# Maxima in two halves of heads, with exponentials among the last scores; normalisation on GpSimd; the gate's first layer in bf16 parts on TensorE; new engine orders

## The chip, the cores and the metric

One core of a Trainium2 chip. The metric is the device time of one execution in microseconds. Five engines run their own instruction queues in order: TensorE (PE), VectorE (DVE), ScalarE (ACT), GpSimd (POOL) and SyncE (SP), which here only issues the DMAs. They meet at semaphores.

## What is computed

Sixteen items (B = 16), each a matrix of 256 positions by 256 features, go through four residual steps:

```python
x = x + einsum(x, W0[subject]) + b0[subject]              # a linear layer chosen per item
x = x + zX*lap_x(x) + zY*lap_y(x) + zR*x*(1 - x)          # a Laplacian step
# attention, 16 heads of 16: q, k_self, v_self from side, k, v of the past from x
score_prev = where(mask, q @ k.T, -inf) / 4               # 256 x 256 per head
score_self = sum(q * k_self) / 4                          # one more column
weights = softmax(concat(score_prev, score_self))
x = x + (weights[..., :-1] @ v + weights[..., -1:] * v_self) @ Wo + bo
# three experts, dense 256 -> 1024 -> 256 with relu: s0, s1 shared, eo chosen per item
w = softmax(relu(concat(eo[:, 0], s0[:, 0], s1[:, 0]) @ g1) @ g2)
x = x + eo*w[0] + s0*w[1] + s1*w[2]
```

The gate g1 sees position 0 alone: a vector of 768 against a 768 x 256 matrix.

## The kernel before

The work is features on partitions, two chunks of 128 (C = 2), 256 positions in the free dimension. A float32 product is made in three matmuls of split operands (hi·hi, hi·lo, lo·hi, function `product`, lines 488 to 490). Scores are bf16 products of stacked parts: `q_rows` and `k_rows` hold three-part splits of q and k in bands of 16 rows, placed there by DMAs (`place`, line 386), with a mask row and, for the second pass, three rows with minus the maximum.

The heads are gone through twice. Stages S0 to S15 (line 586) make scores with queries on partitions, and VectorE takes each row's maximum (line 930). After S15 the maxima are joined with the self score (933), subtracted (935), transposed on TensorE (`mT`, 591), split in three bf16 rows by VectorE (941 to 944) and brought into `q_rows` by three DMAs (421). Stages E0 to E15 (597) make scores less maximum with keys on partitions; ScalarE takes the exponential, once in float32 (777) and for even heads once more in float16 (781); for odd heads VectorE makes the float16 part (950). What is left, `prob_lo`, is made by VectorE for odd heads (951) and by GpSimd for even ones (1136). The products with V, `attend(h)` (539, 540), stand three heads later: E_h is followed by `attend(h - 3)`, and `pvend` holds the last three. `attend(8)` reuses the banks of the first eight heads and waits for `pv_freed`, which VectorE raises after it has summed a bank (stage `half`, 961 and 963). Stages `norm` and `att` normalise (970 to 974); `aT` transposes, `wo` projects.

The experts are H0 to H11 (a hidden block of 128x512, 12 matmuls) and P0 to P11 (12 matmuls into the output banks), four of each per expert. After an H, ScalarE makes `hid_hi` (821) and VectorE `hid_lo` (1004), and P needs both. After P3, P7 and P11 ScalarE copies the output (801). The third expert is chosen per item: SP loads its first matrix into `raw`, stage `wi_part` splits it (ScalarE 794, GpSimd 1086), then SP loads the second into the same `raw` (`wo_load`, line 370), and `wo_part0` to `wo_part3` split that. Stages gate0 to gate2 form the gate's first layer on VectorE (1014 to 1019); TensorE sums it with ones (655); `relu`, `logits`, `mix`, `scale` follow.

One loop turn holds the front of item i, the attention's second part of item i-1 and experts of items i-1 and i-2. The order in a turn is a list, `BODY`, written out by hand: a front order with `STEP` saying what follows each stage. All engines follow it, VectorE with the later places of `DVE_LATER`. Front stages use two PSUM banks alternately (`front_bank`): a stage waits until the one two places earlier in `USES` has been read, by ScalarE (`freed_act`) or VectorE (`freed_dve`). TensorE's turn reads, from S0: S0 S1 P1 S2 S3 H3 S4 S5 P2 S6 S7 H4 S8 S9 P3 S10 S11 H5 S12 S13 P4 S14 S15 H6 mT P5 H7 P6 E0 E1 H8 E2 P7 E3 E4 H9 E5 E6 P8 E7 to E10 H10 E11 E12 P9 E13 E14 H11 E15 P10 pvend x1 P11 q aT gate ks logits lap wo vs kp vp H0 self H1 P0 H2. ScalarE's `wi_part` stands behind S1, `wo_load` behind S3, `wo_part0` behind H5.

Before the loop VectorE splits the linear weights, and in the first item's turn the shared experts' weights are loaded and split in eight pieces (`SHARED_AT`).

Of the kernel before, what the change touches and what calls it, by code (L numbers as in the profile page):

```python
# [80 lines left out]
DVE_BODY = list(BODY)  # L87
for name, later in DVE_LATER.items():
    DVE_BODY.remove(name)
    DVE_BODY.insert(DVE_BODY.index(later) + 1, name)  # L90
LAGS = (EARLY + ATTENTION[:FIRST_HALF] + ["x_parts", "w_parts", "s_parts", "x1_parts", "x2_parts", "react", "self"],
        ATTENTION[FIRST_HALF:] + ["half", "norm", "pvend", "att", "aT", "wo", "x3_parts"]
        + [x for stage in ATTENTION[:FIRST_HALF] for x in AFTER.get(stage, []) if x not in ("sum", "self", "store")])
LAG = {x: 0 if x in LAGS[0] else 1 if x in LAGS[1] else 2 for x in BODY}
# [1112 lines left out]
```

## Time and profile before

| | |
|---|---|
| median of 3 runs | 1146.45 us (1146.3 to 1146.51) |
| profiled execution | 1148.39 us, span 1146.8 us |
| TensorE busy | 988.7 us, 86% |
| VectorE busy | 868.9 us, 76% |
| ScalarE busy | 603.8 us, 53% |
| GpSimd busy | 568.5 us, 50% |
| DMA queue's share | 32% |
| mean granted TensorE clock | 0.967 of full |

The chain that ended last is made of TensorE 38%, VectorE 30%, issue 12%, DMA 10%, ScalarE 6%. Read the engine shares first, then the waits of the busiest engine, and then, in order of time, one turn out of the middle: sixteen items make sixteen nearly equal turns, with a first one that has no experts beside it (TensorE's busy tenths there are 5, 5 and 8 in slices two to four, with the clock granted at half for most of it) and a last one that has little else.

### The profile page before, as it was taken

How to read it: one execution, taken by the hardware profiler on the slowest of the kernel's cores; microseconds unless marked ns; L12 is line 12 of the kernel's file. 1: busy time of each engine (PE TensorE's matmuls, PEld its weight loads, DVE VectorE, ACT ScalarE, POOL GpSimd, SP SyncE). 2: the span in 40 equal slices, each digit the busy share in tenths (PEclk: the TensorE clock that was granted, in tenths of full speed). 3: DMA queues.
4: the chain of work that ended last, by engine and by line, in shares of the span. 5: the costliest groups of instructions: out<-in, count | busy, mean ns of one | idle time of the engine just before them, and what ended most of it. 6: DMA issues, size and time to landing. Idle time of an engine off the chain costs nothing.

```text
span 1146.8 us, 27267 instructions
## 1 busy us (share of the span) xinstructions
PE 988.7 (86%) x9456; PEld 922.6 (80%) x9456; DVE 868.9 (76%) x1710; ACT 603.8 (53%) x1177; POOL 568.5 (50%) x432
## 2 busy tenths in 40 slices
PE   4558988998898999889899888989898898989886
PEld 4228888888888888888888888888888888888785
DVE  3576787877778787777878777787877778787733
ACT  3354654646565464656546455655645565554532
POOL 6573636455463645446364544636454463644422
PEclk9559999999999999999999999999999999999988
DMA  4725233251524324152422415242241524223110
GB/s 133 161 74 84 76 70 65 69 92 37 92 74 72 74 61 88 37 92 74 76 80 55 83 37 92 74 80 86 48 80 37 92 74 83 83 55 73 39 46 10
DMA packets 79339, 83.46 MB, mean 73 GB/s; under 512 B 11444, under 2 KB 74708, under 8 KB 79316
## 3 DMA queue, kind: packets, MB, share of 16 engines
q1 hardware_dynamic: 79316, 83.15, 32.0%
q8 instruction: 14, 0.23, 0.1%
q14 instruction: 9, 0.07, 0.0%
HBM read 53.37 MB, written 4.20 MB: 50 GB/s over the span
## 4 chain that ended last, share of the span: by engine, by line
PE 38%; DVE 30%; issue 12%; DMA 10%; ACT 6%; SPq 2%; POOL 1%; DVEq 1%; ACTq 0%; POOLq 0%
DMA k_rows<-prob_lo 7%; PE front L586 4%; DVE prob_hi L950 4%; PE out L488 4%; PE out L489 4%; PE out L490 4%; PE hid L488 4%; PE hid L490 4%; PE hid L489 4%; PE front L597 3%; DVE s_max L930 3%; DMA q_rows<-max_rows 3%; DVE hid_lo L1004 2%; PE front L488 2%; SPq L421 2%
## 5 line engine op out<-in xcount | busy, mean ns | idle before, releaser
L821 ACT ACTIVATE hid_hi<-hid 128x512 fp32r<-128x512 f32 x192 | 114.6, 597 | 251.5 <-PE hid L490 250.8
L488 PE MATMUL out<-hid_hi,exp_hi 128*128 128x256 f32 x768 | 230.1, 300 | 14.7 <-DVE hid_lo L1004 14.6
L1136 POOL TENSOR_TENSOR prob_lo<-prob,prob_hi 128x512 f16<-128x512 f32 x128 | 162.9, 1273 | 137.3 <-ACT prob_hi L781 137.3
L488 PE MATMUL hid<-x_hi,exp_hi 128*128 128x256 f32 x768 | 226.7, 295 | 2.2 <-DVE x_lo L1000 2.2
L930 DVE TENSOR_REDUCE s_max<-front 128x2 f32<-128x512 f32 x256 | 165.2, 688 | 77.0 <-PE front L586 76.0
L489 PE MATMUL out<-hid_lo,exp_hi 128*128 128x256 f32 x768 | 216.8, 282 | 0.0
L490 PE MATMUL out<-hid_hi,exp_lo 128*128 128x256 f32 x768 | 216.5, 282 | 0.0
L489 PE MATMUL hid<-x_lo,exp_hi 128*128 128x256 f32 x768 | 214.5, 279 | 0.0
L490 PE MATMUL hid<-x_hi,exp_lo 128*128 128x256 f32 x768 | 214.4, 279 | 0.0
L1086 POOL TENSOR_TENSOR exp_lo<-raw,exp_hi 128x512 fp32r<-128x512 f32 (+1 forms) x80 | 154.8, 1946 | 104.5 <-ACT exp_hi L794 104.3
L777 ACT ACTIVATE prob<-front 128x512 f32<-128x512 f32 x256 | 146.8, 600 | 63.4 <-PE front L597 61.7
L1004 DVE SCALAR_TENSOR_TENSOR hid_lo<-hid,hid_hi 128x512 fp32r<-128x512 f32 x192 | 131.0, 682 | 48.8 <-ACT hid_hi L821 48.8
L488 PEld LDWEIGHTS out<-hid_hi,exp_hi 128*128 128x128 f32 x768 | 146.1, 190 | 19.5 <-DVE hid_lo L1004 18.2
L488 PEld LDWEIGHTS hid<-x_hi,exp_hi 128*128 128x128 f32 x768 | 145.5, 189 | 3.3 <-DVE x_lo L1000 2.5
L489 PEld LDWEIGHTS out<-hid_lo,exp_hi 128*128 128x128 f32 x768 | 146.5, 191 | 0.0
L490 PEld LDWEIGHTS out<-hid_hi,exp_lo 128*128 128x128 f32 x768 | 146.3, 190 | 0.0
L489 PEld LDWEIGHTS hid<-x_lo,exp_hi 128*128 128x128 f32 x768 | 145.7, 190 | 0.0
L490 PEld LDWEIGHTS hid<-x_hi,exp_lo 128*128 128x128 f32 x768 | 145.0, 189 | 0.0
L950 DVE CAST prob_hi<-prob 128x512 f16<-128x512 f32 x128 | 86.2, 674 | 55.0 <-ACT prob L777 51.4
L597 PE MATMUL front<-q_rows,k_rows 100*128 100x256 bf16 x512 | 100.0, 283 | 27.3 <-DMA q_rows<-max_rows 18.5
L539 PE MATMUL pv<-v_cols,prob_hi 128*128 128x49 bf16 x1024 | 89.6, 187 | 32.2 <-DVE prob_lo L951 19.4
L539 PEld LDWEIGHTS pv<-v_cols,prob_hi 128*128 128x128 f16 x1024 | 72.4, 97 | 50.2 <-DVE prob_lo L951 25.2
(153 smaller groups left out, 2280.7 us busy)
## 6 DMA issues: line engine op xcount, KB each, us to landing
raw<-in_wi SPq DMA_DIRECT2D x16, 1024.0 KB, 4.9
raw<-in_wo SPq DMA_DIRECT2D x16, 1024.0 KB, 5.5
q_rows<-prob_hi SPq DMA_DIRECT2D x96, 128.0 KB, 4.2
k_rows<-prob_lo SPq DMA_DIRECT2D x96, 128.0 KB, 4.6
x_raw<-in_x SPq DMA_DIRECT2D x17, 256.0 KB, 2.7
w_raw<-in_w SPq DMA_DIRECT2D x17, 256.0 KB, 2.8
s_raw<-in_side SPq DMA_DIRECT2D x17, 256.0 KB, 3.5
out<-e_out SPq DMA_DIRECT2D x16, 256.0 KB, 2.2
```

What stands on the lines that cost most here:

```text
L488: nc.tensor.matmul(acc, w_hi, a_hi, start=first, stop=False)
L489: nc.tensor.matmul(acc, w_hi, a_lo, start=False, stop=False)
L490: return nc.tensor.matmul(acc, w_lo, a_hi, start=False, stop=last)
L539: nc.tensor.matmul(acc, prob_hi[:, h % NPROB, at:at + P], v_cols[:, k, h, :], start=(k == 0), stop=False)
L597: last = nc.tensor.matmul(psum[:, k * S:(k + 1) * S], k_rows[0:ROWS_EXP, h, k * P:(k + 1) * P], q_rows[0:ROWS_EXP, h, :], start=True, stop ...
L777: last = nc.scalar.activation(prob[:, h % NPROB, :], psum[:, :], ACT.Exp, scale=SCALE)
L821: nc.scalar.activation(hid_hi[:, s % 2, :], hid_bank[s % 2][:, :], ACT.Relu).then_inc(hid_hi_done, 1)
L930: nc.vector.tensor_reduce(s_max[:, :, h:h + 1], psum, AX_X, ALU.max).then_inc(freed_dve, 1)
L950: linkf(nc.vector.tensor_copy(prob_hi[:, h % NPROB, :], prob[:, h % NPROB, :]))
L1004: nc.vector.scalar_tensor_tensor(hid_lo[:, s % 2, :], hid_bank[s % 2][:, :], 0.0, hid_hi[:, s % 2, :].bitcast(F32), ALU.max, ALU.subtract) ...
L1086: nc.gpsimd.tensor_tensor(exp_lo[:, CHOSEN, first:last], raw[:, at:at + last - first], exp_hi[:, CHOSEN, first:last].bitcast(F32), ALU.sub ...
L1136: nc.gpsimd.tensor_tensor(prob_lo[:, h % NPROB, :], prob[:, h % NPROB, :], prob_hi[:, h % NPROB, :], ALU.subtract).then_inc(prob_split_poo ...
```

## The change

1. *Maxima by halves.* After S7 and after S15 VectorE joins eight heads' maxima with the self score and splits them in three bf16 parts before the transposition (six operations of 128x16). `m0` and `m1` transpose the parts in bf16, ScalarE copies them to `max_rows`, and one DMA per half brings them to `q_rows`. E0 to E4 stand among S11 to S15.
2. *Normalisation.* VectorE keeps the sums and the reciprocal; the addition of v_self and the two multiplications per half go to GpSimd (stages `norm`, `att`).
3. *Gate.* g1 is split once into three bf16 parts, in the first turn (ScalarE and GpSimd, at E8 and E12). `gy` splits the 768 values in three parts on VectorE after the last output copy, and TensorE makes 36 bf16 matmuls of one to three columns instead of four float32 ones of one column.
4. *Moves.* x2b from VectorE to ScalarE; the third part of k is a stage of its own (`k3`) behind `wo`; `self` takes a front bank; `pvend` stands behind x1; `wi_part` stands behind S7, `wo_load` behind S9, `wo_part0` behind H6.
5. *Orders.* `BODY` and `DVE_BODY` are two lists written out.

```diff
+BODY = """
+S4 S5 x_parts H3 S6 w_parts S7 wi_part P2 H4 S8 m0 s_parts P3 S9 wo_load H5 S10 P4
+E0 S11 H6 wo_part0 E1 S12 P5 wo_part1 E2 S13 H7 wo_part2 E3 S14 P6 wo_part3 E4 S15 H8 E5 P7 m1
+E6 E7 H9 P8 E8 E9 H10 E10 half P9 norm E11 E12 H11 E13 E14 P10 E15
+x1 x1_parts react pvend att q P11 gy lap x2_parts ks gate aT relu vs kp logits mix scale wo k3 x3_parts vp self sum
+H0 H1 P0 S0 S1 store H2 S2 S3 P1
+""".split()
+DVE_BODY = """
+S4 S5 x_parts S6 S7 H3 S8 H4 S9 S10 H5 S11 S12 H6 E1 S13 H7 S14 E3 S15 H8 E5 H9 E7 H10 E9 half H11 E11 E13 E15
+x1 x1_parts att gy react lap x2_parts relu aT kp logits mix scale wo k3 x3_parts vp self
+H0 S0 H1 S1 S2 S3 H2
+""".split()
+THIS = "x_parts w_parts s_parts x1 x1_parts react q lap x2_parts ks vs kp k3 vp self S0 S1 S2 S3".split()
+BEFORE = (["m0", "m1", "half", "norm", "pvend", "att", "aT", "wo", "x3_parts", "H0", "H1", "P0", "H2", "P1"]
...
-
-STEP = [("S7", "H4 x_parts"), ("S8", "w_parts"), ("S9", "P3"), ("S10", "s_parts"), ("S11", "H5 wo_part0"),
-        ("S13", "P4 wo_part1"), ("S15", "H6 wo_part2"), ("mT", "P5 H7 P6 gate0 wo_part3"), ("E1", "H8"),
-        ("E2", "P7"), ("E4", "H9"), ("E6", "P8"), ("E10", "half H10"), ("E12", "norm P9 gate1"), ("E14", "H11"),
-        ("E15", "P10 pvend att"), ("x1", "P11 gate2 x1_parts"), ("q", "aT gate relu react"), ("ks", "logits"),
-        ("lap", "mix x2_parts scale wo"), ("vs", "x3_parts"), ("vp", "sum H0 self H1 P0 H2"), ("S1", "P1 wi_part"),
-        ("S3", "H3 store wo_load"), ("S5", "P2")]
-FIRST_HALF = ATTENTION.index("S5") + 1
-DVE_LATER = {"H2": "S1", "H3": "S5", "H4": "S9", "H5": "S13", "H6": "mT", "aT": "relu"}
-AFTER = {name: rest.split() for name, rest in STEP}
-FRONT = ATTENTION[FIRST_HALF:] + EARLY + ATTENTION[:FIRST_HALF]
-BODY = [x for stage in FRONT for x in [stage] + AFTER.get(stage, [])]
...
+                elif name in ("m0", "m1"):
+                    half = int(name[1])
+                    wait_freed_act(sp, i, name)
+                    sp.dma_start(q_rows[ROWS_MAX:ROWS_EXP, half * HALF:(half + 1) * HALF, :], max_rows[:, :]).then_inc(max_placed, 16)
...
+                elif name in ("m0", "m1"):
+                    half = int(name[1])
+                    wait(pe, max_split, 2, i, half + 1)
                     for t in range(C):
-                        last = nc.tensor.transpose(psum[0:H, t * P:(t + 1) * P], s_max[:, t, :], ident[:, :])
...
                 elif name[0] == "E":
                     h = int(name[1:])
-                    if h == 0:
-                        wait(pe, max_placed, 16 * 3, i, 16 * 3)
+                    if h % HALF == 0:
+                        wait(pe, max_placed, 16 * 2, i, 16 * (1 + h // HALF))
                     for k in range(C):
                         last = nc.tensor.matmul(psum[:, k * S:(k + 1) * S], k_rows[0:ROWS_EXP, h, k * P:(k + 1) * P],
                                                 q_rows[0:ROWS_EXP, h, :], start=True, stop=True)
...
+                    wait(pe, y_split, 1, j, 1)
+                    for c in range(C):
+                        acc = out_bank[c]
+                        for e in range(NE):
+                            for k in range(C):
+                                row = (e + 1) % NE * C + k
+                                for n in range(3):
+                                    last = nc.tensor.matmul(acc[:, S:S + 3 - n], g_parts[:, n, row, c * P:(c + 1) * P],
+                                                            y_parts[:, e, k, 0:3 - n], start=((e, k, n) == (0, 0, 0)),
+                                                            stop=((e, k, n) == (NE - 1, C - 1, 2)))
...
+                    for c in range(C):
+                        last = nc.scalar.activation(x2b[:, c, :], react[:, c, :], ACT.Identity, bias=vec[:, c, BO:BO + 1])
+                    last.then_inc(x2b_done, 1)
+                elif name in ("m0", "m1"):
+                    half = int(name[1])
+                    heads = slice(half * HALF, (half + 1) * HALF)
+                    wait_filled(act, i, name)
+                    wait(act, max_placed, 16 * 2, i, 16 * half)
+                    nc.scalar.activation(max_rows[:, :], front_psum(name)[0:3 * HALF, :].bitcast(BF16)[:, 0:S], ACT.Copy).then_inc(freed_act, 1)
+                    wait(act, d_self_done, 2, i, half + 1)
+                    nc.scalar.activation(p_self[:, :, heads], d_self[:, :, heads], ACT.Exp, scale=SCALE).then_inc(p_self_done, 1)
                 elif name[0] == "E":
...
+            def gate_part(n):
+
+                if n == 0:
+                    act.wait_ge(gate_in, 32)
+                else:
+                    act.wait_ge(g_rest, 1)
+                nc.scalar.activation(g_parts[:, n, :, :], g_raw, ACT.Copy).then_inc(g_cut, 1)
...
+                                                       ALU.add, ALU.subtract).then_inc(k_rest_done if c == 0 else freed_dve, 1)
+                elif name == "k3":
                     for c in range(C):
                         wait(dve, k_part_done, 2 * C, i, C + c + 1)
                         last = nc.vector.tensor_tensor(k_parts[2][:, c, :], k_rest[:, c, :], k_parts[1][:, c, :], ALU.subtract)
-                    last.then_inc(freed_dve, 1)
...
-                elif name == "mT":
-                    wait_filled(dve, i, name)
-                    rows = front_psum(name)[0:H, 0:S]
-                    first, second, third = (max_rows[:, n, :] for n in range(3))
-                    linkf(nc.vector.tensor_scalar(first, rows, -1.0, None, ALU.mult))
-                    nc.vector.scalar_tensor_tensor(max_rest, rows, -1.0, first, ALU.mult, ALU.subtract)
-                    linkf(nc.vector.scalar_tensor_tensor(second, rows, -1.0, first, ALU.mult, ALU.subtract))
-                    nc.vector.tensor_tensor(third, max_rest, second, ALU.subtract).then_inc(freed_dve, 1)
+                        nc.vector.tensor_tensor(top, top, own, ALU.max).then_inc(max_done, 1)
+                        wait(dve, max_done, 2, i, half + 1)
+                        linkf(nc.vector.tensor_scalar(first, top, -1.0, None, ALU.mult))
+                        nc.vector.scalar_tensor_tensor(m_rest[:, :, :], top, -1.0, first, ALU.mult, ALU.subtract)
+                        linkf(nc.vector.scalar_tensor_tensor(second, top, -1.0, first, ALU.mult, ALU.subtract))
+                        nc.vector.tensor_tensor(third, m_rest[:, :, :], second, ALU.subtract).then_inc(max_split, 1)
+                        nc.vector.tensor_tensor(d_self[:, :, heads], own, top, ALU.subtract).then_inc(d_self_done, 1)
                 if name[0] == "E" and int(name[1:]) in DVE_PARTS:
...
+                    nc.vector.reciprocal(den[:, :, heads], den[:, :, heads]).then_inc(den_done, 1)
...
+                elif name == "gy":
+                    wait(dve, e_out_done, NE, j, NE)
+                    y = e_out[:, :, :, 0:1]
+                    first, second, third = (y_parts[:, :, :, n:n + 1] for n in range(3))
+                    linke(nc.vector.tensor_copy(first, y))
+                    nc.vector.tensor_tensor(y_rest[:, :, :, :], y, first, ALU.subtract)
+                    linke(nc.vector.tensor_tensor(second, y, first, ALU.subtract))
+                    nc.vector.tensor_tensor(third, y_rest[:, :, :, :], second, ALU.subtract).then_inc(y_split, 1)
...
-                    last.then_inc(gate_relu, 1)
+                    nc.vector.tensor_reduce(gate_v[:, 0:1], out_bank[0][:, S:S + 3], AX_X, ALU.add)
+                    linke(nc.vector.tensor_reduce(gate_v[:, 1:2], out_bank[1][:, S:S + 3], AX_X, ALU.add))
+                    nc.vector.tensor_scalar(gate_h[:, :, :], gate_v[:, :].unsqueeze(2).to_broadcast([P, C, P]), 0.0, None, ALU.max
+                                            ).then_inc(gate_relu, 1)
...
+                    half = 0 if name == "norm" else 1
+                    heads = slice(HALF * half, HALF * (half + 1))
+                    cols = slice(HALF * DH * half, HALF * DH * (half + 1))
+                    wait(pool, den_done, 2, i, half + 1)
+                    wait(pool, own_done, 1, i, 1)
+                    nc.gpsimd.tensor_tensor(att[:, :, cols], att[:, :, cols], v_self[:, :, cols], ALU.add).then_inc(norm_link, 1)
+                    wait(pool, norm_link, 2, i, half + 1)
+                    for t in range(C):
+                        by_head = att[:, t, cols].rearrange("p (h d) -> p h d", d=DH)
+                        last = nc.gpsimd.tensor_tensor(by_head, by_head, den[:, t, heads].unsqueeze(2).to_broadcast([P, HALF, DH]),
+                                                       ALU.mult)
+                    if half == 1:
+                        last.then_inc(att_done, 1)
                 elif name[0] == "E" and int(name[1:]) not in DVE_PARTS:
...
```

## Rows read from the trace of the kernel before

**Rows 1.** The page, busy shares; the source view of L900 (start, first and last).

```profile
PE 988.7 (86%) x9456; PEld 922.6 (80%) x9456; DVE 868.9 (76%) x1710; ACT 603.8 (53%) x1177; POOL 568.5 (50%) x432
...
L900 DVE SCALAR_TENSOR_TENSOR react<-front,z_sb,react x16: 741/743/751, 26.4 to 1029.1; 128x512 f32<-128x512 f32 x16
```

**Rows 2.** Stretches of time (us, busy by engine, granted clock, DMA): mid-run.

```profile
592.00:659.00 67.00, 60.07 (x590) 56.71 (x591) 53.72 (x108) 37.47 (x75) 34.11 (x27) 1.00 0.32 71
```

**Rows 3.** What TensorE waited for: us in total, times, longest us.

```profile
PE pv L539 <- DVE prob_lo L951: 19.4, 18, 1.8
PE front L586 <- DMA k_rows<-prob_lo: 19.4, 16, 9.9
PE front L597 <- DMA q_rows<-max_rows: 18.5, 16, 7.5
PE front L488 <- DVE x_lo L873: 17.8, 16, 2.3
PE out L488 <- DVE hid_lo L1004: 14.6, 16, 1.0
PE pv L539 <- DVE den L963: 12.3, 31, 1.5
PE front L591 <- DVE s_max L933: 10.8, 16, 1.9
PE out L655 <- DVE gate_terms L1016: 6.5, 16, 1.8
```

**Rows 4.** TensorE in order of time: start us, us, instruction (first of each block).

```profile
594.15 0.28 PE L488 MATMUL hid<-x_hi,exp_hi 128*128 128x256 f32 x1
...
595.57 0.29 PE L488 MATMUL out<-hid_hi,exp_hi 128*128 128x256 f32 x1
...
614.06 0.38 PE L597 MATMUL front<-q_rows,k_rows 100*128 100x256 bf16 x2
...
614.48 0.37 PE L488 MATMUL hid<-x_hi,exp_hi 128*128 128x256 f32 x1
...
615.98 0.39 PE L597 MATMUL front<-q_rows,k_rows 100*128 100x256 bf16 x2
```

**Rows 5.** ScalarE in order of time.

```profile
601.49 0.66 ACT L801 ACTIVATE e_out<-out 128x256 f32<-128x256 f32 x2
...
616.18 0.60 ACT L821 ACTIVATE hid_hi<-hid 128x512 fp32r<-128x512 f32 x1 [0.47 <-PE hid L490]
616.67 0.59 ACT L777 ACTIVATE prob<-front 128x512 f32<-128x512 f32 x1
...
643.32 1.91 ACT L794 ACTIVATE exp_hi<-raw 128x2048 fp32r<-128x2048 f32 x1
...
655.58 1.15 ACT L794 ACTIVATE exp_hi<-raw 128x512 fp32r<-128x512 f32 x2 [0.26 <-DMA raw<-in_wo]
```

**Rows 6.** VectorE in order of time.

```profile
610.36 0.55 DVE L961 TENSOR_REDUCE att<-pv 128x128 f32<-128x384 f32 x1
...
611.43 0.68 DVE L1004 SCALAR_TENSOR_TENSOR hid_lo<-hid,hid_hi 128x512 fp32r<-128x512 f32 x1
612.03 0.41 DVE L950 CAST prob_hi<-prob 128x512 f16<-128x512 f32 x1
612.48 0.69 DVE L951 TENSOR_TENSOR prob_lo<-prob,prob_hi 128x512 f16<-128x512 f32 x1
```

**Rows 7.** GpSimd and SP in order of time.

```profile
645.31 4.60 POOL L1086 TENSOR_TENSOR exp_lo<-raw,exp_hi 128x2048 fp32r<-128x2048 f32 x1 [3.13 <-ACT exp_hi L794]
...
650.07 0.39 SPq L370 DMA_DIRECT2D raw<-in_wo  x1
```

**Rows 8.** VectorE and GpSimd in order of time, first turn.

```profile
60.61 2.62 DVE L944 TENSOR_TENSOR max_rows<-prob,max_rows 16x256 bf16<-16x256 f32 x1
...
60.60 2.35 POOL L1080 TENSOR_TENSOR exp_lo<-raw,exp_hi 128x1024 fp32r<-128x1024 f32 x1
```

**Rows 9.** Groups by line: busy us, mean ns.

```profile
L1126 POOL TENSOR_TENSOR v_cols<-beside,v_cols 128x256 bf16<-128x256 f32 x32 | 22.2, 714 | 103.6 <-DVE v_cols L923 103.6
```

More of the change, by code:

```diff
@@ L62 @@
 assert NU % 2 == 0
-ACT_FREES = {"ks", "q", "vs"} | {f"E{h}" for h in range(H)}
+EARLY = ("x_parts", "x1", "react", "lap")
+ACT_FREES = {"ks", "q", "vs", "m0", "m1"} | {f"E{h}" for h in range(H)}
 ACT_ORDER = [x for x in USES if x in ACT_FREES]
 DVE_ORDER = [x for x in USES if x not in ACT_FREES]
-STEP = [("S7", "H4 x_parts"), ("S8", "w_parts"), ("S9", "P3"), ("S10", "s_parts"), ("S11", "H5 wo_part0"),
[5 rows of a table removed]
-FIRST_HALF = ATTENTION.index("S5") + 1
-DVE_LATER = {"H2": "S1", "H3": "S5", "H4": "S9", "H5": "S13", "H6": "mT", "aT": "relu"}
-AFTER = {name: rest.split() for name, rest in STEP}
-FRONT = ATTENTION[FIRST_HALF:] + EARLY + ATTENTION[:FIRST_HALF]
-BODY = [x for stage in FRONT for x in [stage] + AFTER.get(stage, [])]
[L87 to L94, printed above, removed]
+GATE_AT = ["E8", "E12"]
 SHARED_AT = ["vs", "kp", "vp", "S1", "S4", "S7", "S10", "S13"]
@@ L544, in front @@
             def front(name, i):
-                if name == "self":
-                    wait(pe, qk_done, 1, i, 1)
-                    for t in range(C):
-                        for c in range(C):
-                            last = nc.tensor.matmul(pv_bank[0][:, t * H:(t + 1) * H], ksT[:, c, t * P:(t + 1) * P],
-                                                    head_ones[:, c * H:(c + 1) * H], start=(c == 0), stop=(c == C - 1))
-                    last.then_inc(self_done, 1)
-                    return
                 if name == "pvend":
@@ L578, in front @@
                     last = token_major(psum, linear(2), x_hi, x_lo)
+                elif name == "self":
+                    wait(pe, qk_done, 1, i, 1)
+                    for t in range(C):
+                        for c in range(C):
+                            last = nc.tensor.matmul(psum[:, t * H:(t + 1) * H], ksT[:, c, t * P:(t + 1) * P],
+                                                    head_ones[:, c * H:(c + 1) * H], start=(c == 0), stop=(c == C - 1))
                 elif name[0] == "S":
@@ L652, in rest @@
                 elif name == "gate":
-                    wait(pe, gate_terms_done, 1, j, 1)
+                    wait(pe, y_split, 1, j, 1)
                     for c in range(C):
-                        last = nc.tensor.matmul(out_bank[c][:, S:S + 1], gate_terms[:, c * P:(c + 1) * P], ones[:, :], start=True, stop=True)
+                        acc = out_bank[c]
[6 more added lines that the diff above has]
+                                                            stop=((e, k, n) == (NE - 1, C - 1, 2)))
                     last.then_inc(gate_done, 1)
@@ L692, in stage @@
             def stage(name, seq):
-                if name in USE or name in ("pvend", "self"):
+                if name in USE or name == "pvend":
                     front(name, seq)
@@ L924, in front @@
                     last.then_inc(freed_dve, 1)
-                    for c in range(C):
-                        nc.vector.tensor_scalar(x2b[:, c, :], react[:, c, :], vec[:, c, BO:BO + 1], None, ALU.add)
                 elif name[0] == "S":
@@ L955, in front @@
                     wait(dve, pv_done, H, i, HALF * (half + 1))
-                    wait(dve, p_self_done, 1, i, 1)
+                    wait(dve, p_self_done, 2, i, half + 1)
                     heads = slice(HALF * half, HALF * (half + 1))
@@ L1038, in turn @@
                 for name, seq in in_turn(i, DVE_BODY):
-                    if name in USE or name in ("x_parts", "x1_parts", "x2_parts", "react", "self", "half", "norm", "att"):
+                    if name in USE or name in ("x_parts", "x1_parts", "x2_parts", "react", "k3", "half", "att"):
                         front(name, seq)
@@ L1139, in stage @@
                     split_shared(SHARED_AT.index(name))
+                if first and name == GATE_AT[0]:
+                    pool.wait_ge(g_cut, 1)
+                    nc.gpsimd.tensor_tensor(g_raw, g_raw, g_parts[:, 0, :, :], ALU.subtract).then_inc(g_rest, 1)
+                elif first and name == GATE_AT[1]:
+                    pool.wait_ge(g_cut, 2)
+                    nc.gpsimd.tensor_tensor(g_parts[:, 2, :, :], g_raw, g_parts[:, 1, :, :], ALU.subtract).then_inc(g_cut, 1)
             nc.gpsimd.memset(q_rows[:, :, :], 1.0).then_inc(rows_set, 1)
```

137 lines of the change are left out of this document (61 added, 76 removed).

## The prediction

> **What bounds the kernel now.** The page comes first: TensorE is busy for 86% of the span, VectorE for 76%, the other two about half [rows 1]. So the question is what the 14% are in which TensorE issues nothing. The time is made of equal turns: an instruction that every turn holds once, L900, first starts at 26.4 us and last, 15 turns later, at 1029.1 us [rows 1], 66.8 us apart on average. In a window of 67 us in mid-run TensorE is busy 60.07 us at a granted clock of 1.00 [rows 2]; so some 6.9 us of each turn are waits, and 16 turns of them are a tenth of the span. The view of TensorE's waits names them [rows 3]. Each sum over 16 turns, divided: the split of probabilities before the last products with V (`pvend`) 1.2, the k rows' DMA 0.6 (less its longest, 9.9, in the first turn), the maxima's DMA 0.7 (likewise less 7.5), `x2_parts` 1.1, the first hidden split 0.9, `pv_freed` 0.8, the last maximum before the transposition 0.7, the gate's terms 0.4. With the smaller ones that is the 6.9. No engine is full; each wait is one chain that comes in late, and a new order is worth what its own chains leave.
>
> The change aims at the maxima (0.7 and 0.7), `pvend` (1.2) and the gate (0.4). I therefore walked one turn of the new order on paper, block by block, with durations from the rows.
>
> **Block lengths.** TensorE [rows 4]: a block of 12 float32 matmuls lasts 1.42 between two such blocks (0.12 each), 1.50 when a head follows; a head's pair and its eight products `attend` 0.42; I give the pair alone 0.15 to 0.2, so the products 0.03 each, and two S heads 0.37. ScalarE [rows 5]: 0.60 for a 128x512 piece, the next begins 0.49 later, and it begins 0.20 after TensorE's block has ended. VectorE [rows 6]: hid_lo 0.60 to the next start, cast 0.45, prob_lo 0.69 to its end, one bank's sums 0.55 and about 0.1 for the denominators.
>
> **Part by part.** *Removed from VectorE:* the gate's terms, x2b, the normalisation. VectorE idles 13 us per turn already [rows 2], so this is no gain by itself. *Added to TensorE:* 36 narrow bf16 matmuls for four float32 ones. The trace has no bf16 matmul of 1 to 3 columns. Nearest are the 49-column products at 0.03, so 1.0 us; the upper bound is the float32 pitch of 0.12, 4.3 us [rows 4]. I take the former, same type and same weight load, less 0.5 for the four that go: +0.5. The bf16 transpositions, two for one, add 0.1. Together +0.6 per turn (bounds 0.2 and 4.0), all on TensorE's own path. *ScalarE* takes two copies of maxima (from nothing to 0.6, a full piece; nearest is half of the pair of output copies, 0.33; I take 0.4) [rows 5] and x2b; it is busy 37 of 67 us, and only its order matters. *GpSimd* takes the normalisation, six operations of at most 0.71, the length of a 128x256 one [rows 9], some 3.3 us; it is busy 34 of 67 us.
>
> **Waits in the new order, with what lies behind each.**
> (a) *The chosen expert's load.* `wi_part` moves from behind H2 to behind S7; the reload of raw and `wo_part0` follow from it, and on ScalarE `wo_part0` stands ahead of E1, whose bank E2 needs. From the end of H3 on TensorE: 0.20, H3's activation 0.50, `w_parts` 0.52, wi_hi 1.91 [rows 5], GpSimd's exp_lo 0.08 and 4.60, SP 0.16 [rows 7], landing 5.5 (from SP's issue to ScalarE's start) [rows 5, 7], wo_hi 0.53, E1's exponential 0.60, hand-over 0.05: 14.65. TensorE has in between S6, S7, P2, H4, S8, m0, P3, S9, H5, S10, P4, E0, S11, H6, E1, S12, P5: 12.1. Wait 2.55. P3's own wait (hid_lo of H3 stands behind the maxima on VectorE, 0.8) lies inside it. In the kernel before this load started some seven microseconds earlier against S0 and cost ScalarE 0.26 [rows 5].
> (b) *E7* needs the bank of m1, whose copy stands on ScalarE behind the output copies of P7: 0.20 + 0.66 + 0.4 against 0.15 + 0.42 of cover: wait 0.65.
> (c) *attend(8)*, behind E11, needs the first half's sums. VectorE's order is H10, E9, half. From the end of H10: 0.20 + 0.60 + 0.07 + 0.60 + 0.45 + 0.61 + 0.65 = 3.2; cover E10, P9, E11 2.1; with the second bank 0.5 later the wait is 1.55.
> (d) *attend(11)*, behind E14, needs E11's split, and VectorE has H11 ahead of E11. From H11's end: 0.20 + 0.60 + 0.07 + 0.60 + 0.45 + 0.69 + 0.05 = 2.66 against E13 and E14, 0.6: wait 2.05. All of TensorE behind E14 is queued. This wait depends on nothing upstream. In return `pvend` stands behind x1 (1.5 of cover) and its 1.2 go.
> (e) *x1 to S0.* Zero is the first matmul of x1. P11 ends at 5.05, its copies at 6.1; `gy` at 7.25, as GpSimd's normalisation is beside it; gate 7.3 to 8.3 (wait 0.3), aT to 8.65. VectorE then has react's two operations of 0.69, as prob_lo with two SBUF inputs [rows 6], against GpSimd's remaining multiplication and a q_rest of 1.15 (a quarter of the 4.60), to 10.1, then lap's 0.74 [rows 1]: bank free at 10.85, so `vs` waits 2.2. `wo` waits 0.35 for ak_lo. Then kp, logits, mix, scale, wo, k3 and x3_parts follow one another on VectorE to 20.0, while TensorE is through `self` at 18.2: H0 waits 1.85, P0 0.3. Sum 5.0, against 3.0 before (k rows, `x2_parts`, first hidden split, gate).
> Sum 11.8. My blocks add to 59.7 per turn where the trace gives 60.4 with the additions; the missing 0.7 is cover, so 11.1. Net per turn: 11.1 - 6.9 + 0.6 = +4.8 us.
>
> **First turn and end.** The first turn has no experts' work beside it, and its 7.5 us for the maxima's DMA are bare: halving hides most of transposition and transfer behind S8 to S15, -8. Against it stand g1's three ScalarE pieces and two 128x1536 GpSimd operations, by the 2.35 us for 1024 columns [rows 8] 3.5 us each, among the exponentials: +5. Net -3 (bounds -8 and +6). The tail exchanges waiting for the gate's terms for gy and relu: nothing.
>
> **Sum.** 15 turns hold both halves of the work: 15 x 4.8 = 72. The profiled execution took 1148.39 with a span of 1146.8; the runs' median is 1146.45, and I add to that: 1146.5 + 72 - 3 = 1215.5.
>
> **A port between VectorE and GpSimd.** L944, a 16x256 subtraction with two SBUF inputs, lasted 2.62 in the first turn; it began 0.01 behind a GpSimd operation of 2.35 and ended 0.28 after it [rows 8]. The short operations on one half's maxima are of this kind. In my walk (zero is S0) GpSimd's p_lo ends at 8.5, the first of them right after, the fourth operation of the split would begin at 9.05, and GpSimd's 4.60 exp_lo of wi is ready at 9.0.
> The Trainium skill, "SBUF — State Buffer", section "Who interferes with whom", says that a VectorE instruction with two SBUF inputs and a GpSimd instruction that reads SBUF contend, and that the later one fully blocks; by that rule the whole 4.6 us are lost, and it speaks against more work on GpSimd. The trace agrees for an operation of 2.35 us.
>
> **Rivals.** *The walk holds*: 1195 to 1235, chance 0.40. *The maxima's split is caught behind exp_lo*: m0 and P3 come 4.6 later, the load's wait (a) vanishes in it, net +2.6 per turn, 1255 (1235 to 1275), chance 0.17; against it: 0.05 us decide. *Milder*: VectorE and ScalarE get ahead while TensorE waits in (c) and (d), so that (e) costs no more than before (3.0) and part of (a) goes: +2 to +3 per turn, 1185 (1150 to 1195), 0.18. *Faster*: the point is 6.3 us of waits per turn. That needs two of (a), (c), (d) gone, for instance if the load lands sooner and E2's bank is free. With (a) and (b) gone, (c) and (d) no more than before's 0.8, (e) 3.0: 3.8 of waits, -2.5 per turn, 1106; half-way 1125. For it speaks that the 1.2 of `pvend` and the 1.4 of the maxima do go; against it that (d) alone is 2 by a queue order that nothing upstream changes. Chance 0.22 for 1095 to 1144. *No change*, within 0.2% (2.3 us, about what a measurement can tell): 0.03.
>
> **Numbers.** Slower 0.40 + 0.17 + 0.18 = 0.75, same 0.03, faster 0.22. The range goes from 1130 to 1260: below it lies most of the faster case, 0.14, above it a third of the caught case, 0.06.
>
> **What would show it.** In TensorE's waits: pv behind VectorE's prob_lo (d) near 2 us per turn, pv behind den (c) 1.5, an E matmul behind ScalarE (a) 2 to 2.6, the maxima's DMA gone. ScalarE's exp_hi behind the DMA raw<-in_wo 1.7 per turn. A VectorE operation on maxima of over 4 us would be the caught case. What would make me wrong: narrow matmuls at a far greater pitch, or a turn of under 67 us, which would mean that chains (a) to (e) overlap rather than add.

## The result and the profile after

The changed kernel takes 1374.55 us (median of 4 runs, 1374.02 to 1375.93) beside 1146.48 of the kernel before on the same chip: a ratio of 1.199, interval 1.197 to 1.201. I had said 1215.5, and at most 1260. The direction was right and the size was not: +228 us where +69 was forecast.

The page after: busy shares, and the row of granted clocks in 40 slices.

```profile
PE 1111.1 (81%) x10000; PEld 1034.3 (75%) x10000; DVE 873.7 (64%) x1663; ACT 633.3 (46%) x1259; POOL 628.3 (46%) x529
...
PEclk9558999898898989999898999989989898999988
```

TensorE has 6% more instructions and 12% more busy time than in [rows 1]. In the kernel before the granted clock is 9 tenths or more from the fourth slice to nearly the end, a mean of 0.967; here eights stand all through it, and the mean is 0.881. The turn, from one L931 (the old L900) to the next, went from 66.6 to 81.9. These two facts already say that something multiplies: TensorE is slower at the work it had before.

What TensorE waited for, after (us in total, times, longest), to be read against [rows 3].

```profile
PE front L592 <- DVE m_parts L972: 65.2, 16, 4.2
PE pv L541 <- DVE den L992: 35.3, 31, 4.5
PE hid L490 <- DVE x_lo L1018: 30.4, 15, 2.2
PE pv L541 <- DVE prob_lo L980: 28.4, 18, 1.8
PE front L490 <- DVE react L931: 20.7, 14, 1.5
PE front L586 <- DVE s_max L960: 18.3, 34, 1.0
...
PE front L599 <- DMA q_rows<-max_rows: 2.7, 2, 1.6
```

The maxima's DMA is gone (18.5 to 2.7), and `pvend`'s wait with it; the first line is new and the largest, 4.1 in each turn. It is m0, waiting for the parts of the first half's maxima. VectorE and GpSimd in order of time in one turn out of the middle:

```profile
611.76 1.05 DVE L967 TENSOR_TENSOR s_max<-s_max,s_self 128x16 f32<-128x16 f32 x1
...
613.15 0.17 DVE L971 SCALAR_TENSOR_TENSOR m_parts<-s_max,m_parts 128x16 bf16<-128x16 f32 x1
613.35 4.45 DVE L972 TENSOR_TENSOR m_parts<-m_rest,m_parts 128x16 bf16<-128x16 f32 x1
...
611.47 1.30 POOL L1114 TENSOR_TENSOR p_lo<-w_raw,p_hi 128x512 fp32r<-128x512 f32 x1 [2.89 <-ACT p_hi L728]
613.28 4.49 POOL L1100 TENSOR_TENSOR exp_lo<-raw,exp_hi 128x2048 fp32r<-128x2048 f32 x1 [0.50 <-ACT exp_hi L822]
```

L972, the last of the split's four operations, takes 0.17 for the second half's maxima. Here it began 0.07 behind GpSimd's 4.49 of wi and ended with it; the first operation, L967, lost 0.88 in the same manner behind p_lo. What follows on TensorE, first the wait, then the first two of P3's twelve matmuls and the head behind them:

```profile
617.86 0.28 PE L592 MATMUL front<-ident_half,m_parts 128*24 128x128 bf16 x2 [4.16 <-DVE m_parts L972]
618.54 0.58 PE L490 MATMUL out<-hid_hi,exp_hi 128*128 128x256 f32 x1 [0.41 <-DVE hid_lo L1022]
618.92 0.42 PE L491 MATMUL out<-hid_lo,exp_hi 128*128 128x256 f32 x1
...
621.27 0.65 PE L586 MATMUL front<-k_rows,q_rows 97*128 97x256 bf16 x2
```

P3 takes 2.73 where the block in [rows 4] took 1.50; its matmuls last 0.41, not 0.28. The stretches of the same turn (from:to in us, its length, busy us of TensorE, its weight loads, VectorE, ScalarE and GpSimd with their instructions, granted clock, DMA share, GB/s):

```profile
610.00:613.30 3.30, 3.30 (x30) 3.22 (x28) 3.07 (x8) 2.92 (x3) 1.33 (x2) 1.00 0.00 0
618.50:621.30 2.80, 2.76 (x13) 2.67 (x14) 1.18 (x2) 0.76 (x3) 1.28 (x1) 0.50 0.02 4
650.10:652.70 2.60, 2.60 (x18) 2.58 (x15) 0.00 (x0) 1.03 (x2) 2.10 (x4) 0.53 0.00 0
655.50:658.00 2.50, 2.50 (x21) 2.41 (x18) 0.83 (x2) 0.98 (x2) 1.16 (x1) 0.59 0.00 0
669.40:673.90 4.50, 4.45 (x24) 4.45 (x25) 2.00 (x6) 3.20 (x7) 2.41 (x2) 0.62 0.23 58
680.10:684.50 4.40, 4.37 (x25) 4.31 (x25) 2.09 (x6) 2.40 (x5) 2.94 (x4) 0.64 0.48 45
610.00:692.00 82.00, 68.40 (x627) 64.26 (x626) 54.37 (x104) 38.75 (x78) 37.20 (x32) 0.90 0.25 58
```

A clock of 1.00 is 2.4 GHz and 0.50 is 1.2; the values between are stretches with both. Each of the five slow ones comes right behind a wait of TensorE: m0 (4.16), attend(8) (1.78 and 0.27), attend(11) (1.82), `vs` (1.48), H0 (2.02). At half clock P3 costs 1.23 more than its 1.50, H11 1.06, P10 0.92, the 24 matmuls of vs and kp 1.61, H0 and H1 1.49; with about 1 at the edges, an estimate from the longer rows beside these blocks, that is 7.3 us of the turn. The other waits of this turn are 1.01 (S14), 0.41 (P3, right behind m0), 0.26 (E7) and 0.24 (gate); behind the 1.01 the matmuls keep their 0.28. So the turn adds up: 66.6, plus waits of 13.45 against 6.9, plus work 0.6, plus 7.3 of half clock, is 81.1 of the 81.9. The remaining 0.8 I have not placed. Over the run 15 turns make 215 of the 228; the rest, 13, lies behind the last L931, where the sixteenth item has its own attend(8) (1.87), attend(11) (1.69) and H0 (2.17). It has no wait at m0. There the same two instructions stand the other way round:

```profile
1267.81 0.17 DVE L972 TENSOR_TENSOR m_parts<-m_rest,m_parts 128x16 bf16<-128x16 f32 x1
...
1268.01 4.60 POOL L1100 TENSOR_TENSOR exp_lo<-raw,exp_hi 128x2048 fp32r<-128x2048 f32 x1 [9.19 <-ACT exp_hi L822]
```

VectorE was 0.20 ahead and nothing was held; instead E2 waited 1.78 for ScalarE, the wait (a) of the prediction.

### The profile page after: what moved, and what is told of

It reads as the page before. It is cut to its first block, busy times and chain, and to the rows that moved or that the text cites. A ratio compares the mean times of both kernels' runs of the same rounds, so it can differ in the third digit from the quotient of the medians.

```text
span 1373.0 us, 28350 instructions
## 1 busy us (share of the span) xinstructions
PE 1111.1 (81%) x10000; PEld 1034.3 (75%) x10000; DVE 873.7 (64%) x1663; ACT 633.3 (46%) x1259; POOL 628.3 (46%) x529
## 4 chain that ended last, share of the span: by engine, by line
PE 51%; DVE 21%; issue 14%; ACT 8%; DMA 2%; POOL 1%; DVEq 1%; SPq 0%; ACTq 0%; POOLq 0%
PE hid L490 7%; PE out L490 6%; PE hid L491 6%; PE hid L492 6%; PE out L492 5%; PE out L491 5%; PE front L586 4%; PE front L599 3%; PE front L490 3%; DVE prob_hi L979 3%; DVE s_max L960 3%; PE front L491 2%; PE front L492 2%; DVE hid_lo L1022 2%; DVE react L927 2%
## 5 line engine op out<-in xcount | busy, mean ns | idle before, releaser
L490 PE MATMUL hid<-x_hi,exp_hi 128*128 128x256 f32 x768 | 249.5, 325 | 30.5 <-DVE x_lo L1018 30.4
L490 PE MATMUL out<-hid_hi,exp_hi 128*128 128x256 f32 x768 | 244.4, 318 | 6.6 <-DVE hid_lo L1022 6.5
L491 PE MATMUL hid<-x_lo,exp_hi 128*128 128x256 f32 x768 | 231.3, 301 | 0.0
L492 PE MATMUL out<-hid_hi,exp_lo 128*128 128x256 f32 x768 | 230.7, 300 | 0.0
L492 PE MATMUL hid<-x_hi,exp_lo 128*128 128x256 f32 x768 | 229.7, 299 | 0.0
L490 PEld LDWEIGHTS hid<-x_hi,exp_hi 128*128 128x128 f32 x768 | 165.3, 215 | 34.0 <-DVE x_lo L1018 32.1
L491 PEld LDWEIGHTS hid<-x_lo,exp_hi 128*128 128x128 f32 x768 | 165.4, 215 | 0.0
L492 PEld LDWEIGHTS hid<-x_hi,exp_lo 128*128 128x128 f32 x768 | 162.4, 211 | 0.0
L541 PE MATMUL pv<-v_cols,prob_hi 128*128 128x49 bf16 x1024 | 93.8, 193 | 63.9 <-DVE den L992 35.3
L980 DVE TENSOR_TENSOR prob_lo<-prob,prob_hi 128x512 f16<-128x512 f32 x128 | 135.6, 1060 | 4.4
L586 PE MATMUL front<-k_rows,q_rows 97*128 97x256 bf16 x512 | 99.1, 293 | 32.0 <-DVE s_max L960 18.3
```

The costliest lines, as they stand in the source:

```text
L490: nc.tensor.matmul(acc, w_hi, a_hi, start=first, stop=False)
L491: nc.tensor.matmul(acc, w_hi, a_lo, start=False, stop=False)
L492: return nc.tensor.matmul(acc, w_lo, a_hi, start=False, stop=last)
L541: nc.tensor.matmul(acc, prob_hi[:, h % NPROB, at:at + P], v_cols[:, k, h, :], start=(k == 0), stop=False)
L586: last = nc.tensor.matmul(psum[:, t * S:(t + 1) * S], q_rows[0:ROWS_MAX, h, t * P:(t + 1) * P], k_rows[0:ROWS_MAX, h, :], start=True, stop ...
L980: nc.vector.tensor_tensor(prob_lo[:, h % NPROB, :], prob[:, h % NPROB, :], prob_hi[:, h % NPROB, :], ALU.subtract).then_inc(prob_split_dve, 1)
```

## The experiments

Two accounts of the size. **Waits and clock**: the waits cost what they last, m0's most of all by GpSimd's long subtraction, and each then costs again, as TensorE's clock is at half for the block behind it. **Rivals**: the clock follows some other part of the change (more narrow matmuls), or has no price of its own; and, for the second half of the runs, that the parts themselves (not their order) cost the time.

**1. The long subtraction in four.** GpSimd's 128x2048 for wi becomes four of 128x512, same place.

```diff
-                    split_chosen(0, C * F, 1, i)
+                    wait(pool, chosen_hi, PARTS, i, 1)
+                    for n in range(4):
+                        at = slice(n * C * F // 4, (n + 1) * C * F // 4)
+                        last = nc.gpsimd.tensor_tensor(exp_lo[:, CHOSEN, at], raw[:, at], ...)
```

> The changed kernel, with GpSimd's subtraction for wi (128x2048, 4.5 us) issued as four of 128x512. Theory P (the fourth operation on the maxima is shut out of the port for as long as one GpSimd instruction lasts): L972's counterpart lasts at most 1.3 us instead of 4.45, the wait of m0 falls from 4.2 to about 1 us per turn, and about 40 us go (some of it comes back as a wait of E2 for the chosen expert's load): 1320 to 1340. Rival (the operation is late for another reason, or a queue of GpSimd operations holds the port as long as one long one): L972 stays over 4 us and the time within 5 us of 1374.

Measured 1330.07, ratio 1.160 (1.157 to 1.164). The long subtraction is the cause of m0's wait: with it in four, the median L972 takes 0.18 and the wait fell from 65.2 to 19.0.

```profile
PE front L599 <- ACT prob L797: 22.2, 18, 3.3
...
PE front L592 <- DVE m_parts L972: 19.0, 16, 3.0
```

Some 18 of these 46 us were handed back by the first line (3.9 in the changed kernel): the wait (a) of the prediction for the chosen expert's load, 1.3 to 1.4 per turn, which the longer one had hidden. The turn went from 81.9 to 78.5.

**2. VectorE's order before attend(8) and attend(11).**

```diff
-... E7 H10 E9 half H11 E11 E13 E15
+... E7 E9 H10 half E11 H11 E13 E15
```

> The changed kernel, with VectorE's order E9 before H10 and E11 before H11. Theory Q (queue order makes the waits (c) and (d)): the wait of the products with V for VectorE's prob_lo, 28.4 us in all, falls under 8, that for the denominators from 35.3 to about 20. Without a clock effect that gives 45 us: 1330. With theory C (a wait of about 2 us is followed by a stretch at half the granted clock, which costs 1 us more) 70 us: 1300, and two of the five half-clock stretches of a turn are gone. Rival: the same microseconds come back as waits of x1 or vs, time within 10 us of 1374.

Measured 1290.1, 1.1255 (1.1222 to 1.1288). The wait for prob_lo is gone and the one for den is 12.2 instead of 35.3, so some 50 us of waits; the time fell by 84. More came back than was waited for.

**3. Idle matmuls in the five waits.** 30, 13, 13, 10 and 14 single-pass matmuls whose results nobody reads, ahead of m0, attend(8), attend(11), `vs` and H0 (those of attend(11) wait first for H11 to be split, as they use its bank).

```diff
+            def fill(bank, n):
+                for _ in range(n):
+                    nc.tensor.matmul(bank[:, 0:S], lin_hi[:, 0, 0:P], lin_hi[:, 0, 0:S], start=True, stop=True)
```

> The changed kernel, with idle matmuls on TensorE ahead of its five long waits in each turn (30 before m0's transposition, 13 before attend(8), 13 before attend(11), 10 before vs, 14 before H0; 128x256 float32, results overwritten). They compute nothing that is used and take no longer than the wait. Theory C (the granted clock falls because TensorE stands still in the waits, and that costs 7 us per turn): the mean granted clock goes from 0.88 to 0.95 or more and the time to about 1270 (turn 75 us). Rival W (the clock falls for another reason, such as the bf16 and narrow matmuls, and the waits cost only themselves): clock unchanged, time 1374 to 1400.

Measured 1289.86, 1.1253 (1.1217 to 1.1288), clock 0.972: 20 us above the 1270 expected. No data came earlier by the edit, TensorE was given more to do, and 85 us went. Its row of clocks is like that of the kernel before:

```profile
PEclk9559999999999999999999999999999999999988
```

That rules out the change's own matmuls as what lowers the clock: they are all there.

**4. Runs 1 and 2 together.** 

> The changed kernel with both e1's four pieces and e2's VectorE order. If the two causes are separate they add: 1374 - 44 - 84 = 1246. If both worked through one shared stretch (a common wait that either of them uncovers), less: 1270 to 1290. Theory C adds nothing of its own here.

Measured 1227.15, clock 0.932, in a single execution, so without an interval. The two alone gave 44 and 84 and raised the clock from 0.881 to 0.894 and 0.897; together they gave 147 and 0.051 of clock, so that the simple sum, 1246, was 19 too high. In a turn out of the middle (626 to 645 us) the waits of 0.92, 1.22 and 0.99 in the first half have a clock of 1.00 throughout. Why fewer of the waits at `vs` and H0, which are as long as before, lower it is not shown.

**5. The kernel before, with a late transposition.** Seven more reductions on VectorE ahead of the last maximum, whose results are overwritten. This lengthens one wait in a kernel that has nothing of the change.

```diff
                     if h == H - 1:
+                        for n in range(7):
+                            nc.vector.tensor_reduce(d_self[:, :, n:n + 1], psum, AX_X, ALU.max)
```

> The kernel before, with seven more reductions of S15's scores on VectorE ahead of its last maximum, into columns that are overwritten: mT comes 4.3 us later in each turn and nothing else is changed. W: a turn grows by 4.3, less what cover swallows: 16 x 4.0 = 64, 1211. Theory C: after the wait a stretch at half the granted clock, 1.3 us more per turn: about 1230, mean granted clock about 0.94.

Measured 1226.65, 1.0701 (1.067 to 1.0732), clock 0.929 against 0.967. The wait grew by 60.5 (from 10.8 to 71.3, below), the time by 80. The blocks behind it are at clock 0.50 (635.1 to 640.2 us of the trace), and being longer they cover 12.2 us of the wait for the maxima's DMA, which is 6.3 in place of 18.5.

```profile
PE front L591 <- DVE s_max L936: 71.3, 16, 6.8
```

**6. The same with 34 idle matmuls ahead of the late transposition.**

> e5_before_late (mT's maximum 4.3 us late in the kernel before) with 34 idle matmuls on TensorE ahead of its wait for the maximum, which end before that wait does. Theory C: the granted clock returns to 0.96 or more, the wait as such stays; 20 of the 81 us that e5 lost come back: 1206. Rival W: 1226, as e5.

Measured 1202.5, 1.0485 (1.046 to 1.051), clock 0.970: 24 us less than without them, though the data come no earlier. So a wait of 3.8 more per turn costs 3.8 and then 1.3 to 1.5 by the clock (from the 20 of run 5 and the 24 here, over 16 turns), in a kernel that has nothing of the change. That is the net price: with the 12.2 that the slow blocks cover in run 5 it is 2.0.

**7. GpSimd's subtraction moved.** Run 2, and `wi_part` behind H2 at the end of the turn, `wo_load` behind S7.

```diff
-... S7 wi_part P2 ...  S9 wo_load H5 ...   store H2 S2
+... S7 wo_load P2 ...  S9 H5 ...           store H2 wi_part S2
```

> e2's VectorE order, and wi_part moved to the end of the turn, behind H2, where the kernel before had it (wo_load behind S7); GpSimd's subtraction stays one instruction of 4.5 us. Theory P: m0's wait goes by order alone, as GpSimd is through before the maxima are there: L972 at 0.2 us, m0's wait under 1.0, E2 has no wait for the load. From e2's 1290 that takes 4.2 - 0.8 of waiting and 1.3 of half clock per turn: 1215. Without the clock effect 1238. Rival: exp_lo at the new place delays GpSimd's x_lo and v's split, and the time comes back before S0 or x1: over 1250.

Measured 1273.16, 1.1088 (1.1056 to 1.112): 17 us less than run 2, where 75 were expected. The number is in the rival's range, but not for its reason. The m0 wait fell from 65.3 to 22.8, but the S heads' waits for s_max rose from 18.1 to 47.1. The collision had found another VectorE operation, one of a single column, that takes 0.15 where nothing holds it:

```profile
646.17 3.39 DVE L910 SCALAR_TENSOR_TENSOR z_mid<-z_sb 128x1 f32<-128x1 f32 x1
...
644.92 4.62 POOL L1100 TENSOR_TENSOR exp_lo<-raw,exp_hi 128x2048 fp32r<-128x2048 f32 x1 [5.11 <-ACT exp_hi L822]
```

**8. Also att, react and lap before gy on VectorE, gate behind vs.** 

> As e6_dve_wi, and the bank of lap is read before gy on VectorE (order att, react, lap, gy), with the gate's matmuls behind vs. Theory E (term (e): vs waits for lap behind gy and GpSimd's normalisation): the wait for react, 20.7 us in all, falls under 5 and so do the microseconds behind it in the chain to H0: 1.5 per turn less than e6, 2.5 with the clock: e6 minus 22 to 37 us, near 1180. Rival: H0's wait for x_lo grows by as much, since the gate's chain (gy, gate, relu, logits, mix, scale) is later: e6 within 8 us.

Measured 1225.51, 1.0673 (1.0642 to 1.0704), clock 0.930. The wait for react (20.7) is gone, one of 15.8 for GpSimd's att came in its place, and 48 us went, more than the 22 to 37 expected and again more than the waits' difference.

**9. All parts, all these orders.** Run 8 plus x_parts behind H3 on VectorE, logits ahead of kp, S13 ahead of E1, att ahead of x1_parts.

> All of the change's edits, with other engine orders: e7's, and on VectorE x_parts behind the first half's maxima and H3 (in e7 its one-column L910 stood 3.4 us behind GpSimd's exp_lo), att ahead of x1_parts, S13 ahead of E1, and logits ahead of kp on VectorE and ScalarE. Theory O (the parts of the change cost nothing worth naming, the orders did it): m0's and S6's waits go (1.9 and 1.1 and two half-clock stretches, 4.5 per turn from e7's 71.6), aT's 0.9, S14's 1.0 and 1.2 of H0's 2.0 with a half-clock stretch: a turn of 63 to 65, 1095 to 1130, faster than the kernel before. Rival R (GpSimd and VectorE shut each other out wherever the normalisation and the splits stand, so that each mended wait comes up in another place, as from e1 to e6): a turn of 68 or more, 1170 or more.

Measured 1218.97, 1.0638 (1.0601 to 1.0675). Theory O failed by 90 us and rival R's number, 1170 or more with a turn of over 68, came true (the turn is 71.7). Who stood beside the maxima:

```profile
689.42 1.47 DVE L969 TENSOR_TENSOR s_max<-s_max,s_self 128x16 f32<-128x16 f32 x1
690.92 1.19 DVE L971 TENSOR_SCALAR m_parts<-s_max 128x16 bf16<-128x16 f32 x1
692.14 1.19 DVE L972 SCALAR_TENSOR_TENSOR m_rest<-s_max,m_parts 128x16 f32<-128x16 f32 x1
...
690.81 1.27 POOL L1116 TENSOR_TENSOR x_lo<-x_raw,x_hi 128x512 fp32r<-128x512 f32 x1
692.03 1.27 POOL L1116 TENSOR_TENSOR p_lo<-w_raw,p_hi 128x512 fp32r<-128x512 f32 x1
```

Three short operations in a row, each held for the length of another GpSimd operation: the end of the 4.62 (686.24 to 690.86), then x_lo, then p_lo. 49.6 us of waits for m_parts were left.

**10. Run 9 with the normalisation back on VectorE.** The three operations per half as in the kernel before, behind the sums.

> e8_orders with the normalisation on VectorE, as in the kernel before (norm behind E11, att's part behind its sums). If GpSimd is the better place, VectorE's extra 2.7 us per turn come late for E11's split or for x1_parts and lap: 5 to 15 us slower than e8. If the port makes GpSimd the worse place (its six operations hold VectorE's casts and react up), 5 to 15 us faster.

Measured 1223.34, 1.0664 (1.0646 to 1.0682). The intervals overlap: in this order the two places cost the same as far as these runs can tell. That is two differences that cancel: with VectorE there are waits of 7.3 (for react) and 7.1 (of lap for x_lo) in all that run 9 hasn't, and the clock is 0.929 against 0.915.

**11. Nothing of GpSimd's beside the maxima.** Run 9, `wi_part` one step earlier, all three splits of inputs behind m0, VectorE's x_parts behind S12.

```diff
-S4 S5 x_parts H3 S6 w_parts S7 wo_load P2 H4 S8 m0 s_parts P3 ...   store H2 wi_part S2
+S4 S5 H3 S6 S7 wo_load P2 H4 S8 m0 x_parts w_parts s_parts P3 ...   store wi_part H2 S2
```

> All parts of the change and the orders of e8_orders, in which the m0 wait (49.6 us in all) had moved onto VectorE's own operations on maxima, each blocked 1.2 to 1.5 by one of GpSimd's. Here wi_part stands one step further ahead, before H2, so that its 4.60 subtraction runs from about 683 to 687.8 on e8's clock where the maxima come at 689.4; x_parts, w_parts and s_parts all stand behind m0, and VectorE's part of x_parts behind S12. Theory O (orders decide: GpSimd beside the maxima, and the granted clock that falls after the wait): the m0 wait falls from 3.1 per turn to under 0.7, the first-half matmuls behind it are no longer at half clock (1.2 + 1.2 per turn), a turn is 67 to 69, time 1140 to 1180. Rival R (the change's parts themselves cost it, or the GpSimd subtractions collide with whatever stands on VectorE wherever they are put): the wait appears on another operation, time 1200 or more.

Measured 1173.76, 1.0239 (1.0216 to 1.0262), turn 68.4. The same three operations, and GpSimd's, in this kernel:

```profile
664.52 0.17 DVE L969 TENSOR_TENSOR s_max<-s_max,s_self 128x16 f32<-128x16 f32 x1
664.73 0.17 DVE L971 TENSOR_SCALAR m_parts<-s_max 128x16 bf16<-128x16 f32 x1
664.94 0.18 DVE L972 SCALAR_TENSOR_TENSOR m_rest<-s_max,m_parts 128x16 f32<-128x16 f32 x1
...
658.14 4.59 POOL L1102 TENSOR_TENSOR exp_lo<-raw,exp_hi 128x2048 fp32r<-128x2048 f32 x1 [1.88 <-ACT exp_hi L822]
667.89 1.29 POOL L1116 TENSOR_TENSOR x_lo<-x_raw,x_hi 128x512 fp32r<-128x512 f32 x1 [5.16 <-ACT x_hi L725]
```

The waits for m_parts are 3.3 in all. By order alone the change's parts went from 1374.6 to 1173.8. Rival R is right in part even so: TensorE now waits 16.2 in all for VectorE's prob_lo (1.9 in run 9), as a cast of 0.41 and a subtraction of 0.69 are held behind two of GpSimd's operations that began at 677.10 and 678.32:

```profile
677.25 1.31 DVE L981 CAST prob_hi<-prob 128x512 f16<-128x512 f32 x1
678.59 1.65 DVE L982 TENSOR_TENSOR prob_lo<-prob,prob_hi 128x512 f16<-128x512 f32 x1
```

**12. Run 11 with 14 idle matmuls ahead of H0.** 

> e11_orders2 with 14 matmuls of one 128x128 pass each, whose results nobody uses, ahead of H0's wait, where TensorE idles about 2 us per turn and its clock is half afterwards for H0 and H1 in e8_orders. Theory C (the granted clock is a cost of its own that idle stretches bring): clock of the run up by 0.01 to 0.02 against e11_orders2, 1.0 to 1.5 us per turn less, so 15 to 25 us below e11_orders2. Rival: the added matmuls only take TensorE's time, or the clock falls elsewhere: no difference, or up to 10 us slower than e11_orders2.

Measured 1144.74, 0.9985 (0.9972 to 0.9998). That is 29 less than run 11, a little more than the 15 to 25 expected. The stretch of H0 and H1 in run 11:

```profile
651.00:655.50 4.50, 4.50 (x25) 4.50 (x26) 2.06 (x6) 2.38 (x5) 3.07 (x4) 0.62 0.66 63
```

and in run 12:

```profile
639.60:642.80 3.20, 3.12 (x25) 2.92 (x25) 2.13 (x7) 2.39 (x5) 1.77 (x3) 1.00 0.95 91
```

The same 24 matmuls take 3.1 in place of 4.5. The clock is 1.00 there, not 0.62. With this the change's parts are level with the kernel before: the 0.15% by which it is below is less than what I had called measurable. Most turns take 65.6, every second or third 67.1. The trace shows the difference: both kinds have two waits of 0.85 to 0.87 and 0.83 ahead of one block, and the block behind them is slowed in the long turns alone, here in the turns that begin at 561 and 629:

```profile
602.20:604.60 2.40, 2.40 (x23) 2.18 (x22) 2.33 (x4) 0.59 (x2) 0.89 (x1) 0.69 0.00 0
669.30:671.70 2.40, 2.40 (x27) 2.33 (x27) 2.33 (x4) 0.91 (x2) 0.91 (x1) 1.00 0.00 0
```

So nearly the same waits need not bring the same clock, and a price per wait is an average.

## Why the prediction was wrong

*The step that failed first: the sum had no term for the granted clock.* I read 1.00 in a window of the kernel before and kept every block at its length there, while I was adding waits of 1.5 to 2.6 to each turn. At the trace's own rows: 7.3 us per turn, some 110 us of the 159 that I missed. Run 3, which fills those waits, gives 85 us back; run 6 shows the same price in the kernel before (24 us for a wait grown by 60).

*The second: "0.05 us decide".* The caught split had a chance of 0.17 and happened in fourteen of the sixteen items with the full 4.45; only the first and the last are otherwise. In waits it cost about what the rival said, +2.6 per turn, since (a) vanished in it: the waits of the turn are 13.45 where my sum had 11.1. The walk had the split's fourth operation at 9.05 and GpSimd's 4.60 at 9.0; in the trace it stood 0.07 behind it. A walk made of rounded blocks can't place two starts within 0.1, and such a coincidence repeats in nearly all turns or in none. It deserved near even odds. That this rival's own range, up to 1275, is 100 us below the result is again the clock. I should have noticed too that GpSimd's p_lo meets the same operations (0.88 lost), so that there were two chances to be caught, not one. The rival's +2.6 and the rows' +7.3 on my +4.8 are 14.7 of the measured 15.3.

By the other steps:

| step | said | measured per turn |
|---|---|---|
| (a) E2 for the load | 2.55; none if caught | none; 1.78 in the last item, not caught; 1.3 to 1.4 in run 1 |
| (b) behind m1's copy | 0.65 | 0.26 |
| (c) attend(8) | 1.55 | 1.78 + 0.27 |
| (d) attend(11) | 2.05 | 1.82 |
| (e) gate, vs, wo, H0, P0 | 0.3, 2.2, 0.35, 1.85, 0.3 | 0.24, 1.48, 0, 2.02, 0 |
| 36 gate matmuls | 1.0 | 0.92 |
| copy of maxima on ScalarE | 0.4 | 0.37 |
| normalisation on GpSimd | 3.3 | 3.0 |
| S14 for its bank | not seen | 1.01 |

The walk of queues was good: (c), (d) and (e) are where it put them and within 0.5, but for `vs`. In (c) the half microsecond more is the port again, decided by 0.03 (below): VectorE's last prob_lo ahead of the sums took 1.66, not 0.69. Of (e), 1.48 in place of 2.2 and nothing at wo and P0 fit vs and kp at half clock taking 1.6 longer, which hides the chain behind them; that is argued, no run holds it apart. My -3 for the first turn was wrong in sign: the first L931 comes 2.5 earlier (23.9 against 26.4), but from the first to the second took 73.9 against 70.1 before; a wait of 11.6 for the k rows' DMA stands in that turn (9.9 before).

```profile
646.43 1.66 DVE L980 TENSOR_TENSOR prob_lo<-prob,prob_hi 128x512 f16<-128x512 f32 x1
...
646.40 1.15 POOL L1164 TENSOR_TENSOR prob_lo<-prob,prob_hi 128x512 f16<-128x512 f32 x1 [1.45 <-ACT prob_hi L801]
```

The range ended at 1260 because each case in it was a sum of waits. No case multiplied. The faster rival's point, 6.3 of waits per turn, was sound as far as it went: run 12, whose waits at m0, vs and H0 are gone or under 0.5, is level with before. But its point was a sum of waits too: in run 11 TensorE is idle for 4.8 us of a turn (571.5 to 639.9), under that point, and the run is 2.4% slower than before.

Still open: what decides in run 12 whether two waits of the same length lower the clock, and whether run 11's last wait at H0 can be ordered away rather than filled.

## What to carry to other kernels

A wait on TensorE can have two prices: its own length, and the half clock of the matmuls behind it; whoever adds a wait of a microsecond or two to a turn whose clock is 1.00 should put both in the sum. Where a chain of short VectorE operations feeds TensorE, look for GpSimd's long operations at the same moment, and give them a place where no short one starts. If a wait can't be ordered away, matmuls whose results nobody reads can be worth issuing (85, 24 and 29 us in runs 3, 6 and 12).
